# Local attention in a fused transformer kernel: one order of steps for all jobs, written as a table

## The chip, the cores and the metric

The program runs on one core of one Trainium2 chip. The time is device microseconds of one execution of the whole program, and it is compared as the median of several executions. The core has five instruction queues that run beside one another, each strictly in its own order: TensorE (PE in the rows), VectorE (DVE), ScalarE (ACT), GpSimd (POOL) and SyncE (SP), which here issues the DMAs. They wait for one another by semaphores.

## The reference

Six sublayers follow one another: two levels, each with a cross attention, a second attention and a feed-forward part. The part that changes is the third of level 0, a small transformer of six layers with local attention. Its core, cut to what matters:

```python
def attn_layer(x, Wqkv, qs, ksc, Wo):              # x: (4, 256, 256)
    q, k, v = jnp.split(x @ Wqkv, 3, -1)           # 16 heads of 64
    q = l2norm(q) * qs; k = l2norm(k) * ksc
    q = q * cos * scale + rotate_half(q) * sin * scale
    k = k * cos / scale + rotate_half(k) * sin / scale
    out = local_attention(q, k, v)                 # windows of 64, each looks one back
    return out @ Wo

def ffn_layer(x, g, bln, W1, b1, W2, b2):
    xn = layernorm(x) * g + bln
    a, gate = jnp.split(xn @ W1 + b1, 2, -1)
    return a * gelu(gate) @ W2 + b2

for i in range(6):
    x = attn_layer(shift_tokens(x), Wqkv[i], ...) + x
    x = ffn_layer(shift_tokens(x), ln_g[i], ...) + x
```

`shift_tokens` takes half of the features from the token before.

## The kernel before

The stage is the class `Local`. Its work is cut into 24 jobs, one for each layer l (six) and batch b (four), job j = 4l + b. A job is a batch's 256 tokens, two tiles of 128. It has three parts. `front` turns the shifted input (`features`), projects queries and keys (`proj`, eight steps by tile, section and half), rotates and normalises them (VectorE and GpSimd under `proj`, then `sumsq`, `norm`, `scale_k`), turns them (`turn`, eight) and projects the values (`values`, four). `back` runs 16 heads of attention and the output projection (`wo`, two steps). `gated` is the feed-forward part: `fs`, `f_stats`, `f_scale`, `ft`, six `w1` with three `gate`, and `w2`, two steps.

A head of attention has four steps, made by `Attention.steps`: `front` (scores on TensorE, maxima on VectorE, exponentials on ScalarE), one step later `divide` (VectorE and GpSimd), three steps later `turn` (TensorE transposes, ScalarE copies), and for each two heads an `apply` (the product with the values, then a copy by ScalarE). Scores have two banks of PSUM.

All steps stand in one list, `self.plan`, made in `order`. Each of the five queues walks this list and runs what it has in each step, so the list is the order of every queue. Before, `order` goes through 26 rounds. In round n the `front` of job n, the `back` of job n-1 and the `gated` of job n-2 are taken together and merged by `even`, in proportion to their numbers of steps (24, 23 and 17). The row of heads begins and ends within a round: `steps` is called for each job.

Steps of eight kinds share three general banks of PSUM in turn: a step can begin on TensorE when the step three uses back has been read out (`gen_free`). The feed-forward input is made so: after both `wo` of a job, VectorE adds them to the residual `y`; SyncE, in step `fs`, then copies `y` with its shift into `self.fs` by three DMAs; VectorE, in step `f_stats`, waits for all three:

```python
on.wait_ge(self.fs_in, 3 * j + 3)
on.wait_ge(self.fs_zero, j + 1)
for q in range(2):
    dve.bn_stats(self.fst[:, q, :], self.fs[:, q, :]).then_inc(*self.f_chain.one())
```

The weights of the next layer are loaded in steps `load_front` (queries and keys, two buffers), `load_values` (one buffer) and `load_back` (wo, w1, w2, one buffer each); `shift` copies the next layer's shifted input by two DMAs.

Of the kernel before, what the change touches and what calls it, by code (L numbers as in the profile page):

```python
# [15 lines left out]
B, S, D = 4, 256, 256  # L16
# [3 lines left out]
H = 16  # L20
# [80 lines left out]
def even(*jobs):  # L101

    ticks = max(n for _, n, _ in jobs)
    taken = [0] * len(jobs)
    out = []
    for tick in range(ticks):
        for n, (job, steps, late) in enumerate(jobs):
            start = late * ticks
            due = steps * (tick + 1 - start) / (ticks - start)
            while taken[n] < due:  # L110
                out += next(job, ())
                taken[n] += 1
    for job, _, _ in jobs:
        for more in job:
            out += more
    return out


def round_robin(*jobs):
    jobs = list(jobs)  # L120
    while jobs:
        for job in list(jobs):
            got = next(job, None)
            if got is None:
                jobs.remove(job)
            else:
                yield got
# [1161 lines left out]
DEPTH = 6  # L1289
# [4 lines left out]
FC = -(-FF // P)  # L1294
# [3 lines left out]
class Local(Stage):  # L1298
# [2 lines left out]

    HP = H // 2
    scale = None

    def __init__(self, c, g):
        super().__init__(c)
# [47 lines left out]
    def order(self):  # L1354

        put = self.plan.append
        put(("load_front", 0))
        for b in range(2):
            put(("shift", 0, b))
        put(("load_mask",))  # L1360
        put(("load_values", 0))
        put(("tables", 0))
        for n in range(3):
            put(("load_back", 0, n))
        put(("features", 0, 0))
        put(("shift", 0, 2))
        jobs = [(l, b) for l in range(DEPTH) for b in range(B)]
        for n in range(len(jobs) + 2):
            parts = [(part(*jobs[n - lag]), steps, late) for lag, (part, steps, late) in
                     enumerate(((self.front, 24, 0), (self.back, 23, 0), (self.gated, 17, 0.1)))  # L1370
                     if 0 <= n - lag < len(jobs)]
            even(*parts)

    def front(self, l, b):
        put = self.plan.append
        if b == 2 and l + 1 < DEPTH:
            put(("load_front", l + 1))
        if b == 3 and l + 1 < DEPTH:
            put(("tables", l + 1))
        yield ()  # L1380

        def project(tile, sec):
            for half in range(2):
                put(("proj", l, b, tile, sec, half))
                yield ()
                put(("sumsq", l, b, tile, sec, half))
            put(("norm", l, b, tile, sec))

        def turn(tile, sec):
            for half in range(2):  # L1390
                put(("turn", l, b, tile, sec, half))
                yield ()

        def values(tile):
            for half in range(2):
                put(("values", l, b, tile, half))
                yield ()
        yield from project(0, 0)
        yield from round_robin(project(0, 1), values(0))
        yield from turn(0, 0)  # L1400
        put(("scale_k", l, b, 0))
        yield from round_robin(project(1, 0), turn(0, 1))
        yield from project(1, 1)
        yield from round_robin(turn(1, 0), values(1))
        if b == B - 1 and l + 1 < DEPTH:
            put(("load_values", l + 1))
        put(("scale_k", l, b, 1))
        yield ()
        if (l, b) != (DEPTH - 1, B - 1):
            l2, b2 = divmod(self.job(l, b) + 1, B)  # L1410
            put(("features", l2, b2))
            if l2 == 0 and b2 + 2 < B:
                put(("shift", 0, b2 + 2))
        yield from turn(1, 1)

    def back(self, l, b):
        put, j = self.plan.append, self.job(l, b)
        for steps in self.at.steps(H * j, [(j, h) for h in range(H)]):
            for s in steps:
                put(("attend", s))  # L1420
            yield ()
        for tile in range(2):
            put(("wo", l, b, tile))
            yield ()
        if b == B - 1 and l + 1 < DEPTH:
            put(("load_back", l + 1, 0))

    def gated(self, l, b):
        put = self.plan.append
        put(("fs", l, b))  # L1430
        yield ()
        yield ()
        yield ()
        put(("f_stats", l, b))
        yield ()
        yield ()
        put(("f_scale", l, b))
        yield ()
        put(("ft", l, b))
        yield ()  # L1440
        for mc in range(0, FC, 2):
            put(("w1", l, b, mc))
            put(("w1", l, b, mc + 1))
            put(("gate", l, b, mc))
            yield ()
        if b == B - 1 and l + 1 < DEPTH:
            put(("load_back", l + 1, 1))
        for tile in range(2):
            put(("w2", l, b, tile))
            yield ()  # L1450
        if b == B - 1 and l + 1 < DEPTH:
            put(("load_back", l + 1, 2))
        if l + 1 < DEPTH:
            put(("shift", l + 1, b))

# [135 lines left out]
    def act(self, act):  # L1593
        on = Waits(act)
        for step in self.plan:
            kind, *a = step
            if kind in ("features", "proj", "turn", "values"):
                l, b = a[0:2]
                j, bank = self.job(l, b), self.bank(step)
                par, free = j % 2, self.freed(step)[0]  # L1600
            if kind == "features":
                on.wait_ge(self.gen_full, self.use[step] + 1)
                act.activation(self.xt[:, par, :, :], bank[:, :].rearrange("p (k s) -> p k s", k=KC),  # L1603
                               ACT.Copy).then_inc(*free.one())
            elif kind == "proj":
                tile, sec, half = a[2:]
                tn = 2 * (4 * j + 2 * tile + sec) + half
                on.wait_ge(self.rot_done, 3 * tn + 3)
                on.wait_ge(self.sum_done, tn - 1)
                act.activation(self.t_sq[:, tn % 2, :].rearrange("p (h d) -> p h d", d=LH),  # L1610
                               bank[:, :].rearrange("p (h d) -> p h d", d=LH),
                               ACT.Square).then_inc(*free.one())
            elif kind == "turn":
                tile, sec, half = a[2:]
                src = bank[:, :].rearrange("p (j t) -> p j t", j=4)
                hs, ts = slice(4 * half, 4 * half + 4), slice(tile * P, (tile + 1) * P)
                on.wait_ge(self.gen_full, self.use[step] + 1)
                on.wait_ge(self.at.s_full, H * (j - 1))
                if sec == 0:
                    act.activation(self.q_even[0:64, par, hs, ts], src[0:64, :, :], ACT.Copy)  # L1620
                    act.activation(self.q_odd[64:128, par, hs, ts], src[64:128, :, :],
                                   ACT.Copy).then_inc(*free.one())
                else:
                    act.activation(self.kt[:, par, hs, ts], src, ACT.Copy).then_inc(*free.one())
            elif kind == "values":
                tile, half = a[2:]
                on.wait_ge(self.gen_full, self.use[step] + 1)
                on.wait_ge(self.at.pv_done, H // 2 * (j - 1))
                act.activation(self.v[:, par, tile, half * 512:(half + 1) * 512], bank[:, :],
                               ACT.Copy).then_inc(*free.one())  # L1630
            elif kind == "attend":
                self.at.act_step(act, on, self, a[0])
            elif kind == "gate":
                l, b, mc = a
                on.wait_ge(self.small_in, 3)
                on.wait_ge(self.gen_full, self.use["w1", l, b, mc + 1] + 1)
                for m in (mc, mc + 1):
                    n = FC * self.job(l, b) + m
                    if n >= 2:
                        lb, mo = divmod(n - 2, FC)  # L1640
                        on.wait_ge(*self.freed(("w1", *divmod(lb, B), mo)))
                    act.activation(self.gl[:, n % 2, :], self.bank(("w1", l, b, m))[:, S:2 * S], ACT.Gelu,
                                   bias=self.ffc[:, l, 1, m:m + 1]).then_inc(*self.gelu_done.one())
# [954 lines left out]
```

## Time and profile before

| | |
|---|---|
| median of 3 runs | 4958.12 us (4954.34 to 4961.64) |
| the profiled execution | 4963.8 us, span 4961.9 us |
| granted TensorE clock, mean of the span | 0.967 |
| TensorE busy | 4427.0 us, 89% of the span |
| VectorE, ScalarE, GpSimd busy | 65%, 58%, 38% |
| the stage `Local`, from its first transpose to its last `w2` | 1360 to 3227 us of the span |
| in it: TensorE busy, of 1867 us | 1756.6 us |

The times come from one execution taken by the profiler. A row of the timeline has the start in us, the duration, the engine, the source line and what is written from what; in brackets stands how long the engine sat idle before it and what ended that. A matmul's duration reaches past the start of the next one, since they are pipelined, so what a step costs on TensorE is read from the starts of successive rows. Rows of one kind that follow one another are merged (x4).

### The profile page before, as it was taken

How to read it: one execution, taken by the hardware profiler on the slowest of the kernel's cores; microseconds unless marked ns; L12 is line 12 of the kernel's file. 1: busy time of each engine (PE TensorE's matmuls, PEld its weight loads, DVE VectorE, ACT ScalarE, POOL GpSimd, SP SyncE). 2: the span in 40 equal slices, each digit the busy share in tenths (PEclk: the TensorE clock that was granted, in tenths of full speed). 3: DMA queues.
4: the chain of work that ended last, by engine and by line, in shares of the span. 5: the costliest groups of instructions: out<-in, count | busy, mean ns of one | idle time of the engine just before them, and what ended most of it. 6: DMA issues, size and time to landing. Idle time of an engine off the chain costs nothing. (4 is left out here: it accounts for less than half of the span.)

```text
span 4961.9 us, 85570 instructions
## 1 busy us (share of the span) xinstructions
PE 4427.0 (89%) x31624; PEld 3025.6 (61%) x31624; DVE 3249.4 (65%) x7542; ACT 2896.0 (58%) x5798; POOL 1872.0 (38%) x1876
## 2 busy tenths in 40 slices
PE   5899998989789999999999999859999999669999
PEld 3555555547556666666676666635555555358888
DVE  5677777767565666656656666356777777575555
ACT  2666666668556666666666666426666666523332
POOL 2223222215564545445545444223222222035554
PEclk8999999989899999999999999979999999879999
DMA  5655555500110010100001000056555555011110
GB/s 138 131 103 104 104 113 102 94 24 1 56 39 6 23 45 13 54 15 26 33 14 53 16 32 6 13 126 129 108 103 104 110 109 90 12 53 49 49 48 19
DMA packets 189931, 305.60 MB, mean 62 GB/s; under 512 B 19736, under 2 KB 109752, under 8 KB 187832
## 3 DMA queue, kind: packets, MB, share of 16 engines
q1 hardware_dynamic: 189520, 300.13, 27.3%
q8 instruction: 256, 4.19, 0.4%
q14 instruction: 155, 1.27, 0.1%
HBM read 215.81 MB, written 73.40 MB: 58 GB/s over the span
## 5 line engine op out<-in xcount | busy, mean ns | idle before, releaser
L707 DVE TENSOR_REDUCE xa_m_part<-xa_ring 128x1 f32<-128x512 f32 x2048 | 1319.1, 686 | 506.3 <-PE xa_ring L856 491.0
L633 ACT ACTIVATE xa_ex<-xa_sc 128x1024 f32<-128x1024 f32 x1024 | 991.6, 1022 | 114.2 <-PE xa_sc L844 99.0
L856 PE MATMUL xa_ring<-xa_ks,xa_q_base 48*128 48x512 f32 x2048 | 517.8, 498 | 185.6 <-DVE xa_m_part L707 129.4
L870 PE MATMUL xa_pv<-xa_ex,xa_vs 128*17 128x256 f32 x8192 | 547.8, 385 | 1.3 <-issue 1.3
L856 PEld LDWEIGHTS xa_ring<-xa_ks,xa_q_base 48*128 48x128 f32 x2048 | 201.4, 185 | 517.2 <-DVE xa_m_part L707 432.9
L1036 ACT ACTIVATE lt_p<-lt_bank,lt_stat,lt_rq 128x128 f32<-128x128 f32 (+1 forms) x768 | 365.6, 482 | 215.4 <-DVE lt_stat L1006 210.1
L1570 POOL TENSOR_TENSOR lt_r_qk<-lt_r_qk,lt_t_rot 128x512 f32<-128x512 f32 x192 | 243.2, 1267 | 611.1 <-DVE lt_t_rot L1686 606.1
L844 PE MATMUL xa_sc<-xa_q_base,xa_ks 50*128 50x256 f32 x4096 | 423.0, 302 | 26.4 <-ACT xa_k L605 5.2
L844 PEld LDWEIGHTS xa_sc<-xa_q_base,xa_ks 50*128 50x128 f32 x4096 | 346.8, 187 | 117.5 <-ACT xa_vs L620 24.1
L1023 POOL TENSOR_SCALAR lt_p<-lt_p,lt_stat 128x192 f32<-128x192 f32 x384 | 335.0, 876 | 197.8 <-DVE lt_stat L1013 197.8
L2412 PE MATMUL moe_bank<-moe_xp,moe_wp 128*128 128x512 f32 x1536 | 373.3, 392 | 5.9 <-POOL moe_wp L2240 4.2
L1809 PE MATMUL lt_bank<-lt_wqk,lt_xt 128*128 128x512 f32 x768 | 365.5, 599 | 0.7 <-ACT lt_xt L1603 0.7
L555 POOL CAST xa_kp<-xa_k 128x512 fp32r<-128x512 f32 (+1 forms) x144 | 84.4, 586 | 655.7 <-ACT xa_k L613 314.2
L1577 POOL TENSOR_TENSOR lt_nrm<-lt_nrm,minus_half 128x16 f32<-128x16 f32 x96 | 280.5, 2922 | 122.4 <-DVE lt_nrm L1703 121.2
L2412 PEld LDWEIGHTS moe_bank<-moe_xp,moe_wp 128*128 128x128 f32 x1536 | 281.5, 189 | 59.9 <-issue 4.3
L870 PEld LDWEIGHTS xa_pv<-xa_ex,xa_vs 128*17 128x17 f32 x8192 | 188.7, 97 | 198.6 <-issue 59.6
L2275 ACT ACTIVATE moe_sg<-moe_bank 128x512 f32<-128x512 f32 x128 | 76.5, 598 | 341.1 <-PE moe_bank L2412 341.1
L1610 ACT ACTIVATE lt_t_sq<-lt_bank 128x512 f32<-128x512 f32 x192 | 114.6, 597 | 267.3 <-DVE lt_t_rot L1686 267.3
L1869 PE MATMUL lt_bank<-lt_ft,lt_w 128*128 128x256 f32 x1152 | 262.5, 381 | 1.2 <-DVE lt_ft L1751 1.2
L2246 POOL TENSOR_TENSOR moe_hp<-moe_hh,moe_hp 128x512 fp32r<-128x512 f32 x128 | 166.1, 1297 | 256.7 <-ACT moe_hp L2253 256.7
L976 PE MATMUL lt_bank<-ident,lt_p 128*128 128x128 f32 x1152 | 199.3, 282 | 54.7 <-issue 54.7
L1002 DVE TENSOR_REDUCE lt_stat<-lt_bank 128x1 f32<-128x128 f32 (+1 forms) x768 | 210.5, 315 | 44.2 <-PE lt_bank L967 44.0
(281 smaller groups left out, 8755.1 us busy)
## 6 DMA issues: line engine op xcount, KB each, us to landing
xa_ks<-keys SPq DMA_DIRECT2D x384, 256.0 KB, 9.1
keys<-xa_kp SPq DMA_DIRECT2D x128, 512.0 KB, 3.8
xa_cx<-in_ctx_t SPq DMA_DIRECT2D x64, 512.0 KB, 4.9
lt_wqk<-in_lt_wqkv SPq DMA_DIRECT2D x6, 2048.0 KB, 8.4
lt_w<-in_lt_w SPq DMA_DIRECT2D x6, 1536.0 KB, 6.2
xa_q_base<-xa_m_rows SPq DMA_DIRECT2D x512, 2.0 KB
moe_w<-in_moe_wg SPq DMA_DIRECT2D x64, 128.0 KB, 2.2
moe_w<-in_moe_wu SPq DMA_DIRECT2D x64, 128.0 KB, 2.3
```

Of the source, the lines that this page charges most:

```text
L633: act.activation(x.ex[:, n % x.NE, :, :], x.sc[n % 2][:, :, :], ACT.Exp).then_inc(*x.ex_done.one())
L707: dve.tensor_reduce(x.m_part[:, i % 2, qt, h, ch:ch + 1], x.bank(n + odd), AX.X, ALU.max).then_inc(*x.dve_out.one())
L844: mm = pe.matmul(x.sc[n % 2][:, 2 * odd + pair, :], x.ks[unit % x.NU][rows, 2 * (g % 2) + pair, kt * P:(kt + 1) * P], x.q_base[rows, 2 * g ...
L856: pe.matmul(x.bank(n + odd), x.q_base[rows, pair, b * S + qt * P:b * S + (qt + 1) * P], x.ks[unit % x.NU][rows, pair % 4, ch * 512:(ch + 1 ...
L870: mm = pe.matmul(x.pv[32 * j:32 * j + x.VW, :], x.vs[:, i % x.NV, kt, 4 * g + j, :], x.ex[:, n % x.NE, 2 * (j % 2) + j // 2, :], start=(kt ...
L1023: pool.tensor_scalar(sv, sv, self.stat[:, n % 5, 3, 1:2], None, ALU.mult).then_inc(*self.div_pool.one())
L1036: act.activation(self.p[:, n % 5, to], s[:, at], ACT.Exp, bias=t3[:, 1, q:q + 1], scale=st.scale_of(b, h, slice(q, q + 1)) if st.scale is ...
L1570: pool.tensor_tensor(out, out, self.t_rot[:, t, :], ALU.add).then_inc(*self.rot_add.one())
L1577: pool.tensor_tensor(n[:, 2, :], n[:, 1, :], c.minus_half[:, 0:H], ALU.pow).then_inc(*self.rnorm.one())
L1809: mm = pe.matmul(bank[:, :], self.xt[:, par, k, tile * P:(tile + 1) * P], self.wqk[:, l % 2, k, col:col + 512], start=(k == 0), stop=(k == ...
L1869: mm = pe.matmul(bank[:, gate * S:(gate + 1) * S], self.w1[:, k, gate * FFP + m * P:gate * FFP + (m + 1) * P], self.ft[:, k, :], start=(k ...
L2412: mm = pe.matmul(self.banks[2 * (n % 2) + j][:, :], self.wp[:, wpart, i, j, k * FI:(k + 1) * FI], self.xp[:, xpart, k, at], start=(m == 0) ...
```

## The change

`front`, `back` and `gated` as generators are gone, and so is the merge by `even`. In their place stands `TABLE`: every step of a job with a tick, a number in units of which a job has 24. Step tick + 24 j is its place; all steps of all jobs are sorted by it. The heads of all 24 jobs are one row: `steps` is called once for 384 heads, and head i stands at tick 23.74 + 1.5 i. The loads, `shift` and `features` have ticks as well. Steps of job j reach from tick -2.97 (its first `proj`) to 78.7 (its second `w2`), so steps of up to four jobs are mixed. What each step does is unchanged, but for one wait in `values` on ScalarE.

```diff
+    TICKS, HEADS, FEATURES, SHIFT = 24, 23.74, 18.59, 75
+    LOADS = ((0, "load_front", 2, ()), (0, "tables", 3, ()), (19.5, "load_values", 3, ()),
+             (57.5, "load_back", 3, (0,)), (71, "load_back", 3, (1,)), (75, "load_back", 3, (2,)))
+    TABLE = ((-2.97, "proj", 0, 0, 0), (-0.67, "proj", 0, 0, 1), (-0.47, "values", 0, 0),
+             (0.96, "sumsq", 0, 0, 0), (2.49, "sumsq", 0, 0, 1), (2.65, "norm", 0, 0),
+             (2.65, "proj", 0, 1, 0), (2.97, "turn", 0, 0, 0), (3.94, "proj", 0, 1, 1),
+             (5.45, "values", 0, 1), (5.99, "sumsq", 0, 1, 0), (6.52, "sumsq", 0, 1, 1), (6.67, "norm", 0, 1),
+             (7.08, "turn", 0, 0, 1), (7.24, "proj", 1, 0, 0), (8.08, "scale_k", 0), (10.84, "proj", 1, 0, 1),
+             (11.14, "turn", 0, 1, 0), (11.97, "turn", 0, 1, 1), (12.89, "sumsq", 1, 0, 0),
+             (13.29, "proj", 1, 1, 0), (13.79, "turn", 1, 0, 0), (13.86, "sumsq", 1, 0, 1),
+             (13.87, "norm", 1, 0), (14.83, "values", 1, 0), (15.39, "sumsq", 1, 1, 0),
+             (15.44, "proj", 1, 1, 1), (16.32, "turn", 1, 0, 1), (17.98, "sumsq", 1, 1, 1),
+             (19.05, "norm", 1, 1), (19.64, "scale_k", 1), (21.97, "values", 1, 1), (22.26, "turn", 1, 1, 0),
+             (22.59, "turn", 1, 1, 1), (55.51, "wo", 0), (55.98, "wo", 1), (57.44, "fs"), (58.4, "f_stats"),
+             (60.8, "f_scale"), (62.64, "ft"), (63.5, "w1", 0), (64.21, "w1", 1), (64.22, "gate", 0),
+             (67.01, "w1", 2), (67.02, "w1", 3), (67.03, "gate", 2), (67.56, "w1", 4), (68.55, "w1", 5),
+             (68.56, "gate", 4), (70.65, "w2", 0), (78.7, "w2", 1))
...
-        for n in range(len(jobs) + 2):
-            parts = [(part(*jobs[n - lag]), steps, late) for lag, (part, steps, late) in
-                     enumerate(((self.front, 24, 0), (self.back, 23, 0), (self.gated, 17, 0.1)))
-                     if 0 <= n - lag < len(jobs)]
-            even(*parts)
...
+        timed = []
+        for j, (l, b) in enumerate(jobs):
+            for tick, kind, *a in self.TABLE:
+                timed.append((self.TICKS * j + tick, len(timed), (kind, l, b, *a)))
+            if l + 1 < DEPTH:
+                for tick, kind, when, a in self.LOADS:
+                    if b == when:
+                        timed.append((self.TICKS * j + tick, len(timed), (kind, l + 1, *a)))
+                timed.append((self.TICKS * j + self.SHIFT, len(timed), ("shift", l + 1, b)))
+            if j + 1 < len(jobs):
+                l2, b2 = divmod(j + 1, B)
+                timed.append((self.TICKS * j + self.FEATURES, len(timed), ("features", l2, b2)))
+                if l2 == 0 and b2 + 2 < B:
+                    timed.append((self.TICKS * j + self.FEATURES, len(timed), ("shift", 0, b2 + 2)))
+        heads = self.at.steps(0, [(j, h) for j in range(len(jobs)) for h in range(H)])
+        for i, head in enumerate(heads):
+            timed += [(self.HEADS + self.TICKS * i / H, len(timed) + m, ("attend", s)) for m, s in enumerate(head)]
+        self.plan += [step for _, _, step in sorted(timed)]
...
-                on.wait_ge(self.at.pv_done, H // 2 * (j - 1))
+                on.wait_ge(self.at.pv_done, H // 2 * (j - 2) + H // 4 * (half + 1))
```

## Rows read from the trace of the kernel before

**Rows 1.** Busy time by engine in the whole stage, then in one steady job.
```profile
core 0: us, PE busy (x) PEld busy (x) DVE busy (x) ACT busy (x) POOL busy (x), PEclk, DMA share, GB/s
...
2162.87:2238.42 75.55, 72.24 (x385) 51.02 (x386) 47.06 (x141) 49.32 (x126) 36.88 (x31) 1.00 0.06 20
1360.00:3227.00 1867.00, 1756.55 (x9216) 1232.79 (x9216) 1130.42 (x3372) 1176.93 (x2995) 885.99 (x744) 0.99 0.08 27
```

**Rows 2.** Timeline of TensorE in that job: where it sat idle longest.
```profile
2165.38 0.52 PE L976 MATMUL lt_bank<-ident,lt_p 128*128 128x128 f32 x3 [1.65 <-issue]
...
2176.47 0.52 PE L976 MATMUL lt_bank<-ident,lt_p 128*128 128x128 f32 x3 [0.63 <-issue]
...
2216.07 0.87 PE L987 MATMUL lt_bank<-lt_pt,lt_v 128*64 128x256 f32 x8 [0.58 <-ACT lt_pt L1043]
```

**Rows 3.** Timeline of GpSimd, the same place one job later.
```profile
2235.45 2.93 POOL L1577 TENSOR_TENSOR lt_nrm<-lt_nrm,minus_half 128x16 f32<-128x16 f32 x1 [0.34 <-DVE lt_nrm L1703]
```

**Rows 4.** Timeline after the last `wo`, where nothing else runs.
```profile
3183.81 7.17 PE L1853 MATMUL lt_bank<-lt_wo,lt_ot 128*128 128x256 f32 x32 [0.48 <-ACT lt_ot L1474]
...
3191.02 0.42 DVE L1719 TENSOR_TENSOR x_sb<-x_sb,lt_bank 128x256 f32<-128x256 f32 x1 [3.03 <-PE lt_bank L1853]
...
3192.95 4.60 SPq L1550 DMA_DIRECT2D lt_fs<-x_sb  x1
...
3201.87 0.43 DVE L1731 BATCH_NORM_STATS2 lt_fst<-lt_fs 128x6 f32<-128x256 f32 x1 [10.30 <-DMA lt_fs<-x_sb]
...
3203.08 0.17 DVE L1735 TENSOR_SCALAR lt_frs<-lt_fmv 128x2 f32<-128x2 f32 x1
```

**Rows 5.** Timeline of VectorE in a steady job: the add, then `f_stats`.
```profile
2225.35 0.42 DVE L1719 TENSOR_TENSOR x_sb<-x_sb,lt_bank 128x256 f32<-128x256 f32 x1 [3.47 <-PE lt_bank L1853]
...
2244.95 0.42 DVE L1731 BATCH_NORM_STATS2 lt_fst<-lt_fs 128x6 f32<-128x256 f32 x1
```

**Rows 6.** Timeline of SyncE's DMA issues in that job: first and third of `fs`.
```profile
2225.84 0.67 SPq L1548 DMA_DIRECT2D lt_fs<-x_sb  x1
...
2227.31 4.77 SPq L1550 DMA_DIRECT2D lt_fs<-x_sb  x1
```

**Rows 7.** Timeline of TensorE: a head's scores, a `proj`, the next head.
```profile
2225.15 0.30 PE L965 MATMUL lt_bank<-lt_mask,ident_bf 128*128 128x320 bf16 x1
...
2225.83 1.88 PE L1809 MATMUL lt_bank<-lt_wqk,lt_xt 128*128 128x512 f32 x4
2227.55 0.30 PE L965 MATMUL lt_bank<-lt_mask,ident_bf 128*128 128x320 bf16 x1
```

**Rows 8.** Timeline of TensorE: an `apply`, a head's turn, a `turn`, the next.
```profile
2243.78 0.87 PE L987 MATMUL lt_bank<-lt_pt,lt_v 128*64 128x256 f32 x8
2244.58 0.55 PE L976 MATMUL lt_bank<-ident,lt_p 128*128 128x128 f32 x3
2244.97 0.60 PE L1821 MATMUL lt_bank<-ident,lt_r_qk 128*128 128x128 f32 x4
2245.40 0.30 PE L965 MATMUL lt_bank<-lt_mask,ident_bf 128*128 128x320 bf16 x1
```

**Rows 9.** Timeline of VectorE under one `proj`: first and last of its three.
```profile
2231.38 0.68 DVE L1682 TENSOR_TENSOR lt_r_qk<-lt_bank,lt_tab 128x512 f32<-128x512 f32 x1
...
2232.31 0.41 DVE L1686 TENSOR_TENSOR lt_t_rot<-lt_bank,lt_tab 128x256 f32<-128x256 f32 x1
```

**Rows 10.** Timeline of ScalarE: the square that frees the bank of that `proj`.
```profile
2232.76 0.60 ACT L1610 ACTIVATE lt_t_sq<-lt_bank 128x512 f32<-128x512 f32 x1 [1.21 <-DVE lt_t_rot L1686]
```

**Rows 11.** Timeline of TensorE early in the stage: two idle gaps, and work after one.
```profile
1381.27 0.63 PE L1821 MATMUL lt_bank<-ident,lt_r_qk 128*128 128x128 f32 x4 [3.34 <-DVE lt_r_qk L1712]
1381.73 3.44 PE L1809 MATMUL lt_bank<-lt_wqk,lt_xt 128*128 128x512 f32 x4
...
1451.10 0.52 PE L976 MATMUL lt_bank<-ident,lt_p 128*128 128x128 f32 x3 [2.74 <-issue]
```

**Rows 12.** Busy time and clock right after a 3.34 and a 14.0 us gap.
```profile
1382.00:1385.20 3.20, 3.20 (x6) 1.14 (x5) 1.07 (x3) 1.09 (x2) 1.27 (x1) 0.50 0.02 5
...
3204.90:3211.00 6.10, 4.84 (x13) 3.78 (x14) 1.00 (x2) 0.00 (x0) 0.00 (x0) 0.50 0.00 0
```

**Rows 13.** Page, DMA issues: the load of queries' and keys' weights.
```profile
lt_wqk<-in_lt_wqkv SPq DMA_DIRECT2D x6, 2048.0 KB, 8.4
```

**Rows 14.** The load of the values' weights, line 1519.
```profile
DMA to landing us min/median/max: 5.8/6.0/7.4
```

**Rows 15.** Timeline of TensorE in the round of the last heads: one gap.
```profile
3150.29 0.31 PE L965 MATMUL lt_bank<-lt_mask,ident_bf 128*128 128x320 bf16 x1 [2.23 <-ACT lt_p L1036]
```

More of the change, by code:

```diff
@@ L1367, in order @@
         jobs = [(l, b) for l in range(DEPTH) for b in range(B)]
-        for n in range(len(jobs) + 2):
-            parts = [(part(*jobs[n - lag]), steps, late) for lag, (part, steps, late) in
-                     enumerate(((self.front, 24, 0), (self.back, 23, 0), (self.gated, 17, 0.1)))
-                     if 0 <= n - lag < len(jobs)]
-            even(*parts)
[L1374 to L1454, printed above, removed]
```

## The prediction

> **What bounds the kernel now.** I read the page first, then the busy time of the stage, then TensorE's timeline through one job, then the chain from `wo` to the feed-forward part. TensorE is the bound: of the 1867 us of the stage it is busy 1756.55, and of the 75.55 us of a steady job 72.24 [rows 1]. VectorE, ScalarE and GpSimd have 47, 49 and 37 us of work in a job, so none of them can be the bound by its sum; they can only be late for a single step. All that an order of steps can win in a job is 75.55 - 72.24 = 3.31 us. Most of that sits at two transposes of a head, 1.65 and 0.63 us, and before the last `apply`, 0.58 us [rows 2]. The reader is to see what stands behind the 1.65: a power of 2.93 us on GpSimd [rows 3], behind which the `divide` of a head waits, and with it the head's turn on TensorE. The last 0.58 is the row of heads running out at the end of the round, where a turn, its copy and an `apply` follow one another with nothing between.
>
> **What the change gives.** A head now comes every 1.5 of 24 ticks, that is every 75.55 / 16 = 4.7 us, and not about every tick with a pause between jobs. A head's chain has half as much again in hand, and there is no start and no end of a row within the 24 jobs. So I take the 3.31 us as gone: for the 22 jobs 0 to 21, whose feed-forward part falls among full work, -73 us. What small gaps the new order brings of its own I bound by nothing and by the old 3.31, and take 0.8 a job (+18), near the low end: ScalarE still changes its table around three `gate` steps, now with `features` and both `turn` of the second queries close by, but no step of TensorE there has less to cover it than its like had before. In the first round with heads TensorE had gaps of 2.74 us and less [rows 11]; -4 for these.
>
> **What it costs: `f_stats`.** Here a stall goes to another place. Sorted by ticks, this is TensorE's work from the end of the second `wo` (55.98) on. Ahead of `f_stats` (58.4): scores of head 6, an `apply`, turn of head 3, scores of 7, turn of 4. Behind it: `proj` (1,0,1) of the next job, `turn` (0,1,0), scores of 8, an `apply`, turn of 5, `turn` (0,1,1), scores of 9, turn of 6, and then `proj` (1,1,0). By the starts of successive rows, scores cost 0.68 and a `proj` 1.72 us [rows 7], an `apply` 0.80, a head's turn 0.39 and a `turn` 0.43 [rows 8]. Up to `proj` (1,1,0) that is 4 x 0.68 + 2 x 0.80 + 4 x 0.39 + 1.72 + 2 x 0.43 = 8.5 us.
>
> VectorE walks the same list. In `f_stats` it stops until all three copies of `fs` have landed. How long that takes when nothing else runs is seen after the last `wo`: the add begins at 3191.02, the third copy is issued at 3192.95 and keeps SyncE for 4.60 us, and the statistics begin at 3201.87, released by the DMA after 10.30 us of idling, 10.85 us after the start of the add [rows 4]. In a steady job the issues are the same, 0.49 us after the add, and the third keeps SyncE for 4.77 us [rows 5, 6]; but there `f_stats` ran 19.6 us after the add [rows 5], and hid it all. Now VectorE gets there with only two heads and `scale_k` between. Everything queued behind it on VectorE waits: the rotation of `proj` (1,0,1), the maxima of head 8, `divide` 7. On ScalarE the square of that `proj` waits for the rotation, and behind the square the copies and exponentials. TensorE's first step that needs any of them is `proj` (1,1,0): it is three uses behind `proj` (1,0,1) and takes its bank.
>
> From the moment at which TensorE could go on after `wo`: add 0.20 us later (2225.15 to 2225.35) [rows 5, 7], data 10.85 later, `f_stats` 1.38 (3201.87 to 3203.25) [rows 4], rotation and square 1.98 (2231.38 to 2233.36) [rows 9, 10], together 14.4 us. TensorE arrives after 8.5 us: 5.9 us of idling, 22 times, +130 us. The bounds: were the statistics alone waited for and the rest caught up, 4.6; with ScalarE's queue of copies and exponentials behind, which comes 3 to 4 us late to the bank of `ft` and to head 10, up to 7.
>
> **The clock.** After the gap of 3.34 us the next `proj` took 3.44 us in place of 1.88 [rows 7, 11], and the granted clock stood at 0.50 for 3.2 us; after 14.0 us of idling it was 0.50 for 6.1 us more [rows 12]. That is 1.2 GHz in place of 2.4, and costs half of the time: 1.6 to 3.05 us. A gap of 5.9 us lies nearer the first: 1.6 a job, +35 us. Nothing, if the gap finds the other engines' backlog in its place, is the lower bound.
>
> **A rule that speaks for the other side.** What the row shows is 10.85 us from the add to the statistics, for three copies issued one behind the other [rows 4]. The Trainium skill, "DMA: Bandwidth & Descriptors", section "Anatomy of one DMA — SWDGE (gpsimd) path", gives a fixed cost of about 2 us a DMA; these come by another path, and no run here has a DMA of that one. By 2 us behind a short issue the data would be there before VectorE arrives, and the sum would be that of the first rival below. I go by the row.
>
> **The loads and `shift`.** They are moved in SyncE's queue too. `shift` (two DMAs, like the last two of `fs`) now waits for the second `w2` at tick 78.7 - 72 = 6.7 of the job in which `wo` stands at 7.98; some 10 us of TensorE's work lie between, so SyncE is free again in time, by a few us. In one job of four, `load_front` (2 MB, 8.4 us to landing) [rows 13] and a part of `load_back` wait for the same `w2` and go out ahead of it; then `fs` comes later. Between nothing and 8.4 I take 2.5, five times: +12. `load_values` waits for `values` (1,1) at 21.97, and the next layer's first `values` stands at 23.53: the load takes 6.0 us [rows 14], TensorE's work between about 6. Five times 1 us, +5; at most 7.4 each. The looser wait in `values` costs nothing: it only lets the first half go when its own heads are done, and is needed in the new order since those values are copied before the job two back has had its last `apply`.
>
> **The end.** In job 22's feed-forward part there is no `proj`. TensorE has about 5.8 us up to the scores of head 10, which need the maxima of 8: a gap near 8, where the old round had gaps of 2.23 us and smaller ones [rows 15]: +3. After the last `wo` both orders are the same chain.
>
> **Sum**, against the profile's span of 4961.9 us (execution 4963.8, 0.1% above the median): -73 + 18 - 4 + 130 + 35 + 12 + 5 + 3 = +126 us, so a span of 5088 and a median of 4958.1 + 126 = 5084. A steady job goes from 75.6 to 80.5 us.
>
> **Rivals.** (1) Faster: the copies are in time, and the even row of heads is what counts. -73 + 18 - 4 + 5 = -54, 4904 us. It decides if the gap stays under 2.5 us, that is if the data are there about 7 us after the `wo` and not 11. For it: the row of 10.85 is from the end of the stage alone, where the issue of the third copy is followed by 4.3 us with nothing seen. Against it: the issues alone take 6.2 us in steady jobs too [rows 6]. 0.11. (2) A milder loss: the gap is 4.6 us, the clock stays at 2.4 GHz, no other gaps: -73 - 4 + 101 + 5 = +29 to about +75, 4987 to 5035. 0.17. (3) A heavier one: 7 us and 3.05 of the clock, 2 us of other gaps, 8.4 for `fs` behind loads: -77 + 154 + 67 + 44 + 42 + 10 = +240 at its worst, from +185 on: 5143 and more. ScalarE speaks for it, with 49 us of work that a stop of 6 us squeezes, and table changes; against it, that while TensorE is at half clock the others catch up. 0.12. (4) The two parts cancel to within 0.2% (about what a measurement of this kernel can tell from no change): 0.03.
>
> My forecast has 0.57, and its own range is 5035 to 5143. The range for 8 in 10 takes in part of the milder and of the heavier case: 5005 to 5150. Faster 0.11, same 0.03, slower 0.86.
>
> **What would show it.** `f_stats` on VectorE released by the DMA of `fs`, 5 us or more each of 23 times; a gap of 5 to 7 us on TensorE before a `proj`, and 0.50 of the clock behind it; the gaps at heads' turns gone; TensorE's idle time in the stage up from 110 to over 200 us; a job of 80 to 81 us. I am wrong if the statistics begin at once, or if the gap lies where TensorE has other steps that I have put behind it.

## The result and the profile after

The changed kernel takes 5050.2 us (median of 4 executions, 5041.72 to 5056.61) against 4959.88 for the one before: a ratio of 1.0183, interval 1.0162 to 1.0204. It is slower, as predicted; 5084 was 34 us too much. The profiled execution has a span of 5042.7 us and a mean granted clock of 0.951. The busy shares on its page, and the costliest wait:

```profile
PE 4453.3 (88%) x31624; PEld 3057.0 (61%) x31624; DVE 3218.7 (64%) x7542; ACT 2879.3 (57%) x5798; POOL 1888.4 (37%) x1876
...
L1757 PE MATMUL lt_bank<-lt_wqk,lt_xt 128*128 128x512 f32 x768 | 407.5, 658 | 138.4 <-ACT lt_t_sq L1558 134.7
```

Nearly all of TensorE's idle time in the stage now stands before one kind of step, `proj`, released by ScalarE's square. The same windows as in [rows 1], the steady job, then the stage, with two more for the 4.4 us behind a gap and the 2.2 us after these:

```profile
core 0: us, PE busy (x) PEld busy (x) DVE busy (x) ACT busy (x) POOL busy (x), PEclk, DMA share, GB/s
...
2209.19:2288.10 78.91, 73.75 (x384) 52.56 (x385) 45.46 (x141) 48.58 (x126) 37.59 (x32) 0.95 0.06 19
...
1356.00:3307.00 1951.00, 1778.99 (x9215) 1263.13 (x9216) 1097.75 (x3371) 1159.13 (x2995) 902.51 (x744) 0.95 0.08 25
...
2209.20:2213.60 4.40, 4.40 (x8) 2.23 (x9) 3.97 (x12) 3.88 (x13) 2.37 (x3) 0.50 0.00 0
2213.80:2216.00 2.20, 2.20 (x21) 1.65 (x20) 2.17 (x5) 1.59 (x3) 1.44 (x2) 1.00 0.00 0
```

A job takes 78.91 us where it took 75.55 [rows 1]. TensorE's idle time in the stage is up from 111 to 172 us, and its busy time by 22 us for the same work, part of which is now done at half clock. The timeline of all engines from the add of `wo` to the `proj`:

```profile
2195.62 0.42 DVE L1667 TENSOR_TENSOR x_sb<-x_sb,lt_bank 128x256 f32<-128x256 f32 x1 [3.03 <-PE lt_bank L1801]
...
2197.55 4.62 SPq L1498 DMA_DIRECT2D lt_fs<-x_sb  x1
...
2203.63 0.49 PE L976 MATMUL lt_bank<-ident,lt_p 128*128 128x128 f32 x3
...
2205.88 0.43 DVE L1679 BATCH_NORM_STATS2 lt_fst<-lt_fs 128x6 f32<-128x256 f32 x1 [6.45 <-DMA lt_fs<-x_sb]
...
2208.54 0.60 ACT L1558 ACTIVATE lt_t_sq<-lt_bank 128x512 f32<-128x512 f32 x1 [7.66 <-DVE lt_t_rot L1634]
...
2209.19 3.78 PE L1757 MATMUL lt_bank<-lt_wqk,lt_xt 128*128 128x512 f32 x4 [5.07 <-ACT lt_t_sq L1558]
```

Read it upwards from the last row. TensorE sat idle for 5.07 us until ScalarE's square, which sat behind the rotation, which sat behind the statistics, which sat behind a DMA of `fs`. Before, the statistics began with no wait [rows 5] and the gaps of TensorE were 1.65 us and less [rows 2]. The `proj` behind the gap takes 3.78 us, not 1.88 [rows 7].

In a job with weights to load, SyncE reaches `fs` late. The second DMA of `shift`, a copy of one row, keeps it for 11.20 us. The add of `wo` begins at 1790.47, but `fs` is issued only at 1794.81, and the gap is nearly twice as long:

```profile
1783.50 11.20 SPq L1487 DMA_DIRECT2D lt_xs<-x_sb  x1
1794.81 0.68 SPq L1496 DMA_DIRECT2D lt_fs<-x_sb  x1
...
1805.40 0.43 DVE L1679 BATCH_NORM_STATS2 lt_fst<-lt_fs 128x6 f32<-128x256 f32 x1 [11.11 <-DMA lt_fs<-x_sb]
...
1808.72 3.78 PE L1757 MATMUL lt_bank<-lt_wqk,lt_xt 128*128 128x512 f32 x4 [9.74 <-ACT lt_t_sq L1558]
```

There are four such gaps (9.54 to 10.53 us); the other 18 before a `proj` are 5.07 to 5.76 us. The gap of job 22 is 7.75 us and stands before `ft`.

What the prediction took as a given is why the data need 10 us. The view of the DMA queues, for 10 us from 2196 on in 40 slices of 0.25 us, shows it:

```profile
GB/s 0 0 0 0 0 51 299 174 2 12 16 14 4 14 14 20 23 20 23 23 20 88 23 20 20 20 18 20 21 20 20 18 20 20 18 20 10 0 0 0
```

The first copy (128 partitions, 128 KB) is over in three slices, at up to 299 GB/s. The second (127 partitions, 127 KB) trickles for 7 us at 20 GB/s. The two copies are of nearly the same size, and one runs at a fifteenth of the peak rate of the other.

### The profile page after: what moved, and what is told of

The parts are those of the page before. It is cut to its first block and busy times, and to the rows that moved or that the text cites. A ratio compares the mean times of both kernels' runs of the same rounds, so it can differ in the third digit from the quotient of the medians.

```text
span 5042.7 us, 85583 instructions
## 1 busy us (share of the span) xinstructions
PE 4453.3 (88%) x31624; PEld 3057.0 (61%) x31624; DVE 3218.7 (64%) x7542; ACT 2879.3 (57%) x5798; POOL 1888.4 (37%) x1876
## 5 line engine op out<-in xcount | busy, mean ns | idle before, releaser
L1757 PE MATMUL lt_bank<-lt_wqk,lt_xt 128*128 128x512 f32 x768 | 407.5, 658 | 138.4 <-ACT lt_t_sq L1558 134.7
L1023 POOL TENSOR_SCALAR lt_p<-lt_p,lt_stat 128x192 f32<-128x192 f32 x384 | 348.6, 908 | 403.1 <-DVE lt_stat L1013 401.0
L1757 PEld LDWEIGHTS lt_bank<-lt_wqk,lt_xt 128*128 128x128 f32 x768 | 146.9, 208 | 265.0 <-ACT lt_t_sq L1558 140.9
```

Source lines behind the costliest of these rows:

```text
L1023: pool.tensor_scalar(sv, sv, self.stat[:, n % 5, 3, 1:2], None, ALU.mult).then_inc(*self.div_pool.one())
L1757: mm = pe.matmul(bank[:, :], self.xt[:, par, k, tile * P:(tile + 1) * P], self.wqk[:, l % 2, k, col:col + 512], start=(k == 0), stop=(k == ...
```

## The experiments

The kernel before, run beside them, had medians of 4957.02 to 4963.74 us; each ratio is to its own. Where a kernel is built on another than the changed one, it is said. The edits are cut to what matters: lines that only make a buffer or adapt another count are left out.

**1. The place of `f_stats`.** The prediction's theory is that the new order calls for the copies too early. Two kernels move steps in the table, e1 three of them and e1b `f_stats` alone:

```diff
e1:  -(58.4, "f_stats"), (60.8, "f_scale"), (62.64, "ft")
     +(61.3, "f_stats"), (62.3, "f_scale"), (63.4, "ft")
e1b: -(58.4, "f_stats")
     +(60.0, "f_stats")
```

> The changed kernel with f_stats moved from tick 58.4 to 61.3, f_scale from 60.8 to 62.3 and ft from 62.64 to 63.4; all else as it is. Theory A (VectorE's wait for the three copies of fs is the whole loss): the statistics now stand behind the proj whose bank was waited for, TensorE has 10.2 us of work ahead of them and the data are there after about 10.5. The gap of 5.1 us a job and the 9.5 to 10.5 us of the four jobs with loads go, and with them the proj at half clock (1.9 us a job). Span 5043 - 23 x 5.1 - 4 x 4.6 - 23 x 1.8, about 4870 us, so faster than before the change; a steady job 72 to 73 us. Theory B (mixing four jobs makes other steps late as well, and the copies are only where it shows): other gaps take its place, before ft, w1 or heads' turns, and the time stays at or above the 4960 us of before the change.

> The changed kernel with f_stats alone moved, from tick 58.4 to 60.0: behind the proj (1,0,1), two turn and head 8, but ahead of head 9 and of proj (1,1,0). Theory A: the gap before proj (1,1,0) goes, since its bank is free; but f_scale is ready only 13.5 us after wo and ft is reached after 10.6, so a gap of about 3 us before ft, and one of 1 to 2 us at values (1,0), whose bank waits for the next rotation. 4.3 us a job in two pieces in place of 5.1 and 1.9 of half clock in one: 35 to 55 us faster than the changed kernel, 4995 to 5015 us. Theory B: no more than the change of one gap for another of the same size, 5040 to 5050 us.

e1: 4901.72 us, 0.9879 (0.9857 to 0.9901). e1b: 4975.38, 1.0034 (1.002 to 1.0047). Three steps moved, none by more than 3 ticks, turn a loss of 1.8% into a gain of 1.2%. In e1 TensorE's gaps in a steady job are these (timeline of TensorE; the last row is the like of the first in a job with loads):

```profile
2227.08 0.63 PE L1808 MATMUL lt_bank<-ident,lt_fs 128*128 128x128 f32 x4 [0.41 <-DVE lt_fs L1688]
...
2229.86 3.72 PE L1817 MATMUL lt_bank<-lt_ft,lt_w 128*128 128x256 f32 x16 [0.44 <-ACT lt_v L1577]
...
2670.99 0.84 PE L1808 MATMUL lt_bank<-ident,lt_fs 128*128 128x128 f32 x4 [3.76 <-DVE lt_fs L1688]
```

The wait is not quite hidden, and in the four jobs with loads 3.5 to 3.8 us are left, so e1 missed its expectation by 30 us. In e1b the wait is cut in two, of which these rows show one job; the third row is the first piece in another job, and below them stand windows behind both:

```profile
2188.76 0.63 PE L1808 MATMUL lt_bank<-ident,lt_fs 128*128 128x128 f32 x4 [2.71 <-DVE lt_fs L1688]
...
2192.22 1.98 PE L1777 MATMUL lt_bank<-lt_wval,lt_xt 128*128 128x512 f32 x4 [0.86 <-ACT lt_t_sq L1558]
...
1644.83 0.81 PE L1808 MATMUL lt_bank<-ident,lt_fs 128*128 128x128 f32 x4 [2.78 <-DVE lt_fs L1688]
...
1645.20:1648.40 3.20, 3.20 (x17) 1.99 (x15) 3.10 (x11) 2.20 (x7) 1.58 (x2) 0.50 0.00 0
2188.80:2192.20 3.40, 2.56 (x20) 1.76 (x20) 3.29 (x11) 2.06 (x7) 1.44 (x2) 1.00 0.00 0
```

Together 3.57 us, and behind these two the clock stays up. It does not everywhere: of the 18 gaps of 2.71 to 3.35 us before `ft`, nine are followed by a granted clock of 0.50 and nine are not. The time is 20 us better than the expectation's lower end. The place of the wait is shown; its cause is not.

**2. A copy fewer.** The third copy (one row) is left out, and that row is set to zero; `f_stats` waits for two.

```diff
-sp.dma_start(fs[0:1, 1, P:D], y[P - 1:P, 2 * b, P:D]).then_inc(*self.fs_in.one())
-dve.memset(self.fs[0:1, 0, P:D], 0.0)
+dve.memset(self.fs[0:1, :, P:D], 0.0)
-on.wait_ge(self.fs_in, 3 * j + 3)
+on.wait_ge(self.fs_in, 2 * j + 2)
```

> The changed kernel without the third copy of fs, that of the one row that comes from the tile before (its place is set to zero, so that row of the feed-forward input is left out); f_stats waits for two copies. Theory A1 (the three copies land one behind another and the third comes last, about 2.4 us after the second): the gap shrinks from 5.1 to 2.7 us a job, 2.4 x 23 = 55 us less, and up to 40 us more if the clock is no longer lowered: 4950 to 4995 us. Theory A2 (the third, which keeps SyncE for 4.6 us, is nearly all of the delay): the gap is under 1 us and the time under 4920 us. Theory A3 (a fixed time from the first issue, whatever follows): no change, 5050 us.

5039.12 us, 1.0154 (1.0131 to 1.0177), a gap of 4.95 us in place of 5.07. The timeline:

```profile
2203.77 0.68 SPq L1496 DMA_DIRECT2D lt_fs<-x_sb  x1
2204.49 0.68 SPq L1497 DMA_DIRECT2D lt_fs<-x_sb  x1
...
2213.43 0.43 DVE L1678 BATCH_NORM_STATS2 lt_fst<-lt_fs 128x6 f32<-128x256 f32 x1 [6.27 <-DMA lt_fs<-x_sb]
```

The issue that kept SyncE for 4.6 us is gone, and the statistics begin as late as ever, 8.9 us after the second issue. A1 and A2, which expected a shorter gap, fell. A3 had the number right, but its reason does not stand up to the next runs. This run shows that the 4.6 us were not the delay. They were a symptom, SyncE held by the slow copy ahead, and that is shown by the one-row issue of e7b below.

**3. The slow copy, split, and doubled.** The theory is now: the copy of 127 rows is the wait, since 127 can't be dealt out evenly over the DMA engines. So it is cut in 112 and 15 rows, the same bytes by one DMA more; in e7a for `fs`, in e7b for `shift` too. e10 goes the other way: the 127 rows are copied twice, the second time to a buffer that nobody reads, and `f_stats` waits for both.

```diff
e7a: -sp.dma_start(fs[1:P, :, P:D], y[0:P - 1, 2 * b:2 * b + 2, P:D]).then_inc(*self.fs_in.one())
     +for lo, hi in ((0, 112), (112, P - 1)):
     +    sp.dma_start(fs[lo + 1:hi + 1, :, P:D],
     +                 y[lo:hi, 2 * b:2 * b + 2, P:D]).then_inc(*self.fs_in.one())
e7b: as e7a, and
     -sp.dma_start(xs[1:P, :, :], y[0:P - 1, 2 * b:2 * b + 2, P:D])
     +for lo, hi in ((0, 112), (112, P - 1)):
     +    sp.dma_start(xs[lo + 1:hi + 1, :, :], y[lo:hi, 2 * b:2 * b + 2, P:D])
     -on.wait_ge(self.xs_in[par], 2 * (j // 2) + 2)
     +on.wait_ge(self.xs_in[par], 3 * (j // 2) + 3)
e10: +sp.dma_start(self.spare[1:P, :, :], y[0:P - 1, 2 * b:2 * b + 2, P:D]).then_inc(*self.fs_in.one())
all: -on.wait_ge(self.fs_in, 3 * j + 3)
     +on.wait_ge(self.fs_in, 4 * j + 4)
```

> The changed kernel with its order as it is; only the second copy of fs, of 127 rows, is made as two copies of 112 and of 15 rows. Theory A4 (after the run with two copies: the copy of 127 rows trickles at 20 GB/s through one of the 16 DMA engines, while the one of 128 rows ahead of it is moved at 300 GB/s, and this trickle is the 9.8 us): with 112 rows, a multiple of 16, it is spread; the data are there about 5 us after the first issue, TensorE's gap falls from 5.1 to under 1 us in 19 jobs and from 9.7 to about 5 in the four behind the loads, and the clock stays up in the 19. Time 4880 to 4900 us, faster than before the change with no step moved. Rival (a fixed latency of three or four chained copies): one copy more makes it no better or worse, 5045 to 5060 us.

> As the run with the copy of fs split, and the copy of 127 rows in shift split the same way. Theory: shift's second copy kept SyncE for 4.7 us, and 11 us behind 2.8 MB of weights, which is why fs went out late in four jobs; now those gaps of about 5 us and their half clock go as well: 4 x 6.5 = 25 us less than the run with fs alone, 4855 to 4880 us. Rival (the weights themselves fill the DMA engines, so fs waits behind 2.8 MB whatever its shape): no more than 8 us less.

> The changed kernel with the suspected cost doubled: the copy of 127 rows of fs is made a second time, into a place that nobody reads, and f_stats waits for it too. Theory (a copy of 127 rows moves at 20 GB/s on one DMA engine, some 6.5 to 7 us for 127 KB): the data come 6.5 to 7 us later, TensorE's gap goes from 5.1 to about 12 us in each of 23 jobs: 5050 + 23 x 6.7 = 5205 us, give or take 15. Rival (latency of one more DMA in the chain): 0.7 to 2 us a job, 5065 to 5095 us.

e7a: 4875.01 us, 0.9843 (0.9822 to 0.9864). e7b: 4839.41, 0.977 (0.9752 to 0.9789). e10: 5200.45, 1.0486 (1.0463 to 1.0509), with this in its timeline:

```profile
2276.94 3.78 PE L1760 MATMUL lt_bank<-lt_wqk,lt_xt 128*128 128x512 f32 x4 [11.71 <-ACT lt_t_sq L1561]
```

A second such copy adds 11.71 - 5.07 = 6.64 us to the gap: that is the duration of one, and the time is 5 us below the theory's 5205. The timeline of e7b from the add to the statistics, and its DMA queues from 2258.7 to 2263 (40 slices of 0.11 us):

```profile
2258.21 0.42 DVE L1671 TENSOR_TENSOR x_sb<-x_sb,lt_bank 128x256 f32<-128x256 f32 x1 [3.03 <-PE lt_bank L1805]
...
2258.70 0.68 SPq L1498 DMA_DIRECT2D lt_fs<-x_sb  x1
...
2259.41 1.57 SPq L1500 DMA_DIRECT2D lt_fs<-x_sb  x2
...
2261.03 0.59 SPq L1502 DMA_DIRECT2D lt_fs<-x_sb  x1
...
2262.75 0.43 DVE L1683 BATCH_NORM_STATS2 lt_fst<-lt_fs 128x6 f32<-128x256 f32 x1 [0.72 <-DMA lt_fs<-x_sb]
```

```profile
GB/s 0 0 0 0 0 0 0 0 0 0 0 0 105 291 300 271 215 38 57 191 224 252 224 81 33 5 0 57 81 5 0 0 0 3 2 0 0 0 0 67
...
lt_fs<-x_sb SPq DMA_DIRECT2D x1, 112.0 KB, 2.2
lt_fs<-x_sb SPq DMA_DIRECT2D x1, 15.0 KB, 2.1
```

Three heaps: 128, 112 and 15 KB, the second at up to 252 GB/s. The statistics begin 4.54 us after the add, not 10.26, the one-row issue behind takes 0.59 us, not 4.62, and each copy lands about 2.2 us after its issue. Both parts are still shifted by one row, so it is not the shift that made the copy slow. The windows of e7b, a steady job and 600 us of the stage:

```profile
2269.03:2341.23 72.20, 71.66 (x384) 51.47 (x384) 45.38 (x141) 48.69 (x125) 37.55 (x31) 1.00 0.20 72
...
2200.00:2800.00 600.00, 597.96 (x3201) 430.03 (x3201) 379.15 (x1169) 411.84 (x1049) 314.83 (x259) 1.00 0.09 29
```

TensorE is busy for 597.96 of 600 us at full clock. The job shown is one of the longer; most take 71.7 to 71.8 us. The gaps left by e7a (3.5 to 3.85 us in the four jobs with loads) are gone too, since `shift` no longer holds SyncE. e7b beat its expectation by 16 us: it left out TensorE's idle time before the stage's first transpose, which went from 31.80 us in the changed kernel to 21.06, since the band behind the first `shift` in the queue of SyncE is loaded sooner. e7b is the fastest of all kernels here.

**4. The splits without the early `f_stats`, and without the new order.** e8 is e7b with the table of e1. e9 is the kernel before with the two splits of e7b.

> Both remedies: f_stats at 61.3, f_scale at 62.3, ft at 63.4, and both copies split. If one cause was behind the loss, the second remedy adds little to the first: within 12 us of the run with both copies split, and 15 to 35 us below the 4902 us of the late f_stats alone (the gaps of 3.5 to 3.8 us in four jobs, and 5 us each in the last two feed-forward parts). If the late order itself is worth something more, it is faster than the split alone by over 15 us.

> The kernel before the change with both copies split. Its order hides the copies, so only the last feed-forward part, where TensorE idles 14.0 us, can gain, by about 5 us: 4950 to 4957 us. Against the changed kernel with the same split this gives what the new order is worth by itself: by my term of 3.31 us less 0.8 in 22 jobs, 55 to 75 us.

e8: 4855.62 us, 0.9809 (0.9786 to 0.9833), 16 us slower than e7b, where 12 at most were expected: with quick copies the late `f_stats` costs something. A steady job of e8 has gaps of 0.40 us before `ft` and 0.45 before `w1`; e7b has mostly under 0.2 before `ft` and none before `w1`. e9: 4937.43, 0.9963 (0.9948 to 0.9977), so the slow copies cost the old order 20 us, more than expected (11 of them within the stage, 9 before its first transpose, by the band as in e7b), and the new order alone is worth 4937 - 4839 = 98 us where 55 to 75 were expected. The timeline of TensorE in e9 shows where some of that comes from. The old gap of 1.65 us stands there 24 times, and behind six of them (2228, 2532 and 2836 among them) the clock falls:

```profile
2228.58 0.52 PE L976 MATMUL lt_bank<-ident,lt_p 128*128 128x128 f32 x3 [1.65 <-issue]
2228.93 3.33 PE L1833 MATMUL lt_bank<-lt_wval,lt_xt 128*128 128x512 f32 x4
...
2305.80 0.52 PE L976 MATMUL lt_bank<-ident,lt_p 128*128 128x128 f32 x3 [1.65 <-issue]
2306.16 1.88 PE L1833 MATMUL lt_bank<-lt_wval,lt_xt 128*128 128x512 f32 x4
```

**5. The clock by itself.** TensorE is given work in the gap of the changed kernel: 42 transposes of the identity, read by nobody, before the turn of each job's head 6.

```diff
+if getattr(st, "filler", False) and n >= H and n % H == 6:
+    for i in range(42):
+        pe.transpose(self.t_banks[n % 2][:, 3 * P:4 * P], self.c.ident[:, :], self.c.ident[:, :])
```

> The changed kernel with 42 transposes of the identity, about 4.7 us, put on TensorE ahead of the turn of head 6 in jobs 1 to 23, into unused columns of the bank that this turn writes: work that nobody reads, in place of the idle time before proj (1,1,0). All else waits as it did. Theory C (lowering of the clock after the gap costs 1.6 to 1.9 us a job of its own): the proj takes 1.9 us in place of 3.8, the granted clock of the stage goes from 0.95 to 0.98 or more, and the time falls by 23 x 1.7 = 35 to 40 us, to 5005 to 5020 us, although TensorE does 110 us more of work. Rival: the half clock costs nothing, because TensorE would only wait later for the others' backlog: 5045 to 5060 us.

5022.58 us, 1.0117 (1.0095 to 1.0139): 28 us less than without the filler, short of the 35 to 40 expected. The wait for the data is the same, and in the four jobs with loads a gap of 4.9 to 5.4 us is left, with 0.50 behind it; the granted clock of the span is 0.968 in place of 0.951, and the `proj` takes 1.98 us in place of 3.78:

```profile
2189.60 4.75 PE L976 MATMUL lt_bank<-ident 128*128 128x128 f32 x42
...
2195.21 1.98 PE L1760 MATMUL lt_bank<-lt_wqk,lt_xt 128*128 128x512 f32 x4 [0.53 <-ACT lt_t_sq L1561]
```

**6. The loads.** `load_front`, the 2 MB ahead of `shift` and `fs` in SyncE's queue, goes from tick 0 to 13.

```diff
-LOADS = ((0, "load_front", 2, ()), (0, "tables", 3, ()), ...
+LOADS = ((13, "load_front", 2, ()), (0, "tables", 3, ()), ...
```

> The changed kernel with load_front alone moved, from tick 0 to tick 13 of the third job of each layer, so that it goes out behind fs and not ahead of shift and fs. Theory (the four gaps of 9.7 to 10.5 us come from shift waiting behind 2 MB of weights): these four fall to about 5.5 us, 4 x 4.5 = 18 us less, 5025 to 5038 us. Rival (they come from the w2 weights, which still go ahead of shift): under 6 us less, 5044 to 5055 us.

5015.94 us, 1.0111 (1.0094 to 1.0127): 34 us less than the changed kernel, where 12 to 25 were expected. In the timeline of TensorE the gap of a job with loads is that of any other:

```profile
2438.54 3.65 PE L1757 MATMUL lt_bank<-lt_wqk,lt_xt 128*128 128x512 f32 x4 [5.18 <-ACT lt_t_sq L1558]
```

Four gaps shorter by 4.4 to 5.3 us are some 19 us, and the spans of the two profiled executions differ by 5042.7 - 5022.1 = 20.6. The rest of the 34 us isn't in the profiled execution, which is the slowest of the four of e5 (its granted clock is 0.952, that of the others 0.956 to 0.957), and stays unexplained.

**7. The row of heads begun anew.** On top of e7b, the heads begin anew in each job, 1.2 ticks apart, and both `wo` come 3 ticks earlier.

```diff
-heads = self.at.steps(0, [(j, h) for j in range(len(jobs)) for h in range(H)])
-for i, head in enumerate(heads):
-    timed += [(self.HEADS + self.TICKS * i / H, ...
+for j in range(len(jobs)):
+    for i, head in enumerate(self.at.steps(H * j, [(j, h) for h in range(H)])):
+        timed += [(self.HEADS + self.TICKS * j + 1.2 * i, ...
```

> The kernel with both copies split and the new table, but with the heads of each job as a row of their own again (20 steps, 1.2 ticks apart, with wo moved from ticks 55.51 and 55.98 to 52.5 and 52.97). It parts the gain of the new order, 98 us between the two kernels with split copies, into what the one even row of heads gives and what the table gives. Theory (the end and the new start of the row cost 0.58 to 1.65 us at the places where rows of before show them, and the power on GpSimd in between): 1 to 2.5 us a job come back, 4862 to 4900 us. Rival (the table gives it all, since norm and heads no longer meet on GpSimd): under 10 us slower than the 4839 us with one row.

4995.29 us, 1.0065 (1.005 to 1.008): 156 us slower than e7b (146 by the two ratios), far from what was expected. Its timeline of TensorE has gaps that e7b lacks, all at the two ends of a row; with one of 0.23 us they make 5.0 us a job, and its TensorE is also busy for 73.41 us of a job, not 71.66, with the clock at 0.98:

```profile
2195.12 0.31 PE L965 MATMUL lt_bank<-lt_mask,ident_bf 128*128 128x320 bf16 x1 [1.82 <-ACT lt_p L1036]
...
2219.34 0.87 PE L987 MATMUL lt_bank<-lt_pt,lt_v 128*64 128x256 f32 x8 [1.16 <-ACT lt_pt L1043]
...
2243.99 0.31 PE L965 MATMUL lt_bank<-lt_mask,ident_bf 128*128 128x320 bf16 x1 [1.83 <-ACT lt_p L1036]
```

The table was written for an even row, and here it meets another; so this is what the row and the table give together, and no price of the row alone.

## Why the prediction was right, step by step

The direction, the place and the mechanism were right. The runs price the two halves of the sum apart. By the stage (first transpose to last add), in the profiled executions: before 1867.6, changed 1952.2, e9 1856.3, e7b 1761.0 us. So the order is worth 1761.0 - 1856.3 = -95; the slow copies cost the new order 1952.2 - 1761.0 = +191 and cost the old one 1867.6 - 1856.3 = 11. Together -95 + 191 - 11 = +85. The prediction had -59 and +185, which is +126, and nothing for the 11. By the medians the change cost 92 us against 4958.1.

- **The gain of the order** (-73, +18, -4): the term that was mis-sized. Idle time went down from 101 us in e9 (1856.3 less 1755.1 busy) to 30 in e7b (1761.0 less 1731.2), that is 71 of the 73. But the new order brought no small gaps: the +18 wasn't there. And TensorE's busy time fell by 24 us for the same work, which I had at nothing. About 10 of them are the clock behind the old gap of 1.65 us: a job of e9 in which it falls takes 77.22 us and the next 75.54, and there are six of these. That is in the row that I used ([rows 1] has 0.99 in the stage), but the one job that I read had 1.00. The other 14 are some 0.6 us a job at full clock (72.24 us busy in a job of e9, 71.66 in one of e7b); why it is less stays open.
- **The gap before `proj`**: 5.9 us predicted, 5.07 to 5.76 found, at the `proj` predicted. The data came 10.26 us after the add, not 10.85, and TensorE arrived after some 8.7 us, not 8.5.
- **The clock**: 1.6 us a gap, +35: too small. The `proj` behind a gap takes 3.78 us in place of 1.88, but the half clock outlasts it. Behind the 22 gaps it stands at 0.50 for 3.2 to 6.2 us, 98.5 us together, which costs half of that: 49 us, or 2.2 a gap. I had taken the price from the gap of 3.34 us in [rows 11]. The filler gave back 28, less what it cost itself.
- **`fs` behind the loads**: +12 as five times 2.5 us. They are four, and each is over 4 us: some 19. I had `fs` wait behind the loads themselves. But e7b, which splits `shift`'s copy and leaves the loads where they are, has no such gap; and e5, which moves only `load_front`, has 5.18 to 5.24 us in these jobs, like the others. Either cure does it: the slow copy held SyncE because the weights were ahead of it.
- **`load_values`** (+5): nothing; from 1750 to 3000 the list of waits has no TensorE wait but that of `proj`. **Job 22**: a gap of 7.75 for the predicted 8, though before `ft` and not before the scores of head 10. The gap of the last job is 14.00 us before and 13.86 after, the same in both orders as said. Some 6 us of it are the slow copies' in either order: e9 has 7.62 there and e7b 7.63.
- **The signs to look for**: a job of 78.91 us for 80 to 81, idle time of 172 us for over 200. Both miss by the small gaps and by 0.8 us of the large one. In the job two more errors cancel: the work is 71.66 us as in e7b, not 72.24, and the clock takes 2.2, not 1.6; 71.66 + 5.07 + 2.2 = 78.9. `f_stats` waits for the DMA in every job, as said.
- **The sum**: its errors cancel in part. The costs were put at +185 and are +191, although the gap was taken too long, the clock too cheap and the last job at nothing. By the stage the forecast is 126 us for 85, so 41 too much: 36 from the gain of the order, 11 from the slow copies in the old one, less 6 from the costs.
- **Rival 1** (the copies in time, 4904 us, decided by data after about 7 us) was the right question with the wrong constant: with data after 4.5 us the program takes 4839. It fell here since the 10 us are real, and the prediction took them rightly from the row. What it did not ask is why. It weighed the fixed cost of about 2 us that the Trainium skill gives for another path against the row, and saw only that they disagree. The row of e7b (2.2 us to landing for 112 KB) agrees with that figure, and so the disagreement was the hint that one copy was of another kind.

The kind is told by the traces: 127 partitions at 20 GB/s, 128 at 299 and 112 at 252, in one queue. The Trainium skill, "DMA: Bandwidth & Descriptors", section "Why a DMA increments its semaphore by 16 and not by 1", has a rule for it: a DMA is spread over as many engines, up to 16, as divide its slowest dimension on both sides, so 128 or 112 partitions go over 16 and the prime number 127 over one. The trace agrees: 127 partitions move at a fifteenth of the peak rate of 128, and 112 at up to 252 GB/s of its 299. That it is one engine is the page's; the runs show the rate, and that the split removes the wait. The busy share of the DMA engines fits it: while the second copy runs it is 0.06 of the core's 16 engines, about one sixteenth:

```profile
2198.60:2200.50 1.90, 1.90 (x8) 0.91 (x7) 0.76 (x4) 1.90 (x9) 1.12 (x2) 1.00 0.06 16
```

Still open: the looser wait in `values` was not tried by itself, nor was the power on GpSimd that the prediction puts behind the old gap of 1.65 us; and the price of the even row alone (experiment 7) is not told apart from its table.

## What to carry to other kernels

When a new order pulls a consumer towards its DMA, read the time from issue to data in the trace, and then ask why it is what it is: a slack of 19.6 us had hidden a copy that ran at a fifteenth of its neighbour's peak rate, and two copies split made a loss of 1.8% into a gain of 2.3%. A copy shifted by one row has 127 partitions: cut it in 112 and 15. And count small gaps of TensorE with what the clock takes behind them, over several jobs rather than one.

## What the hardware did that was not expected

- A copy within SBUF of 127 KB over 127 partitions takes about 7 us at 20 GB/s; of 128 KB over 128 partitions less than 1 us at up to 299 GB/s. Made twice, it takes 6.64 us more.
- SyncE's next issue behind such a copy is held, though it is of one row: 4.62 us, and 11.20 behind weights being loaded; behind the copy of 15 rows it takes 0.59.
- Behind the 22 gaps of 5.07 to 10.53 us TensorE is at 1.2 GHz (granted clock 0.50) for 3.2 to 6.2 us. In e9 a gap of 1.65 us did so six times of 24, and left 2.4 GHz the others; in e1b gaps of 2.71 to 3.35 us did so nine times of 18. Gaps of one length do not have one outcome.
